# A Mamba block and a linear attention block on one core: the four taps of a depthwise convolution as products of TensorE, and shared buffers

## The reference

```python
# first block (D=256, DI=512, N=16, RANK=64, TAPS=4)
shift, scale, gate = split(silu(c) @ ada_w.T + ada_b, 3)
xn = layernorm(x) * (1 + scale) + shift
x_in, z = split(xn @ in_proj_w.T, 2)
u = silu(depthwise_causal_conv(x_in, conv_w) + conv_b)   # 4 taps along the rows
dt_r, B, C = split(u @ x_proj_w.T)
dt = softplus(dt_r @ dt_proj_w.T + dt_proj_b)
h[t] = h[t-1] * exp(dt[t] * A) + dt[t] * u[t] * B[t]     # 512 x 16 states
y = (h . C + u * D) * silu(z)
x1 = x + gate * (y @ out_proj_w.T)
# second block: linear attention with 8 heads
q, k, v = LN(x1) @ Wq, LN(x1) @ Wk, LN(x1) @ Wv
y = softmax(q, in a head) @ (softmax(k, over the rows).T @ (v * mask))
out = x1 + silu(LN(y) * (1 + s) + b) @ W_out + b_out
```

## Time and profile before

| | |
|---|---|
| median of 3 runs | 570.05 us (568.83 to 570.15) |
| the profiled execution | 569.01 us, span 567.2 us |
| mean granted TensorE clock in it | 0.901 of 2.4 GHz |
| VectorE busy | 514.6 us, 566 instructions |
| GpSimd busy | 453.0 us, 318 instructions |
| TensorE busy | 437.9 us, 2456 instructions |
| ScalarE busy | 408.6 us, 897 instructions |

### The profile page before, as it was taken

The page is one execution under the profiler, slowest core; times in us unless marked ns, Lnnn a source line. Parts: engine busy times, 40 slices in busy tenths (PEclk is TensorE's granted clock), DMA queues, the critical chain, the costliest instruction groups (busy, mean ns, idle before and its releaser), DMA issues. The chain is left out here.

```text
span 567.2 us, 7391 instructions
## 1 busy us (share of the span) xinstructions
PE 437.9 (77%) x2456; PEld 361.2 (64%) x2456; DVE 514.6 (91%) x566; ACT 408.6 (72%) x897; POOL 453.0 (80%) x318
## 2 busy tenths in 40 slices
PE   8967666769789787768688678768787777866887
PEld 7646445657676676656576667647674666755776
DVE  2479899999999999999999999999999999999753
ACT  2693677668865998578966999488966988486533
POOL 4049969989998889979998889978997989985121
PEclk8988777896789798998989898998899898779899
DMA  9294032201430044001440045011440045000001
GB/s 269 66 326 125 3 114 85 102 4 54 159 112 0 29 151 154 14 19 40 159 131 1 28 151 165 2 29 43 147 129 1 10 151 166 2 0 20 0 1 37
DMA packets 22366, 45.38 MB, mean 80 GB/s; under 512 B 3685, under 2 KB 13557, under 8 KB 22329
## 3 DMA queue, kind: packets, MB, share of 16 engines
q1 hardware_dynamic: 22328, 44.92, 24.3%
HBM read 42.52 MB, written 2.39 MB: 79 GB/s over the span
## 5 line engine op out<-in xcount | busy, mean ns | idle before, releaser
L530 POOL TENSOR_TENSOR hs<-dtu,Br 128x1024 f32<-128x1024 f32 x127 | 297.0, 2362 | 8.5 <-DMA Br<-bc_rows 8.5
L722 ACT ACTIVATE ring<-dt,Aneg 128x256 f32<-128x256 f32 x512 | 212.9, 465 | 72.6 <-DVE hs L957 68.7
L950 DVE TENSOR_TENSOR_SCAN ring<-ring,hs 128x1024 f32<-128x1024 f32 x97 | 221.4, 2282 | 5.8 <-ACT ring L722 5.4
L1298 PE MATMUL sums<-ident,hs 128*128 128x128 f32 x1024 | 150.7, 303 | 36.3 <-DVE hs L957 36.0
L1298 PEld LDWEIGHTS sums<-ident,hs 128*128 128x128 f32 x1024 | 134.4, 158 | 48.3 <-DVE hs L957 44.7
L957 DVE TENSOR_TENSOR hs<-ring,Cr 128x1024 f32<-128x1024 f32 x97 | 118.8, 1225 | 3.3
L539 POOL TENSOR_TENSOR hs<-hs,Cr 128x1024 f32<-128x1024 f32 x31 | 73.2, 2360 | 42.1 <-DVE hs L950 42.1
L950 DVE TENSOR_TENSOR_SCAN hs<-ring,hs 128x1024 f32<-128x1024 f32 x31 | 70.3, 2269 | 0.0
L1366 PE MATMUL PY<-wqkvo,xT 128*128 128x256 f32 x168 | 46.6, 428 | 0.0
L1293 PE MATMUL sums<-ident,uD 128*128 128x128 f32 x64 | 15.5, 333 | 35.2 <-DVE ygT L964 35.2
L1366 PEld LDWEIGHTS PY<-wqkvo,xT 128*128 128x128 f32 x168 | 37.5, 223 | 6.6
(11 more groups left out here) (218 smaller groups left out, 694.1 us busy)
## 6 DMA issues: line engine op xcount, KB each, us to landing
Br<-bc_rows SPq DMA_DIRECT2D x32, 512.0 KB, 5.1
Cr<-bc_rows SPq DMA_DIRECT2D x32, 512.0 KB, 4.2
xg<-in_x SPq DMA_DIRECT2D x8, 256.0 KB, 2.9
out<-fin SPq DMA_DIRECT2D x7, 256.0 KB, 4.2
hs<-in_ada_wT SPq DMA_DIRECT2D x3, 512.0 KB, 4.6
win<-in_in_wT SPq DMA_DIRECT2D x2, 512.0 KB, 6.1
hs<-in_W_emb SPq DMA_DIRECT2D x2, 512.0 KB
gate<-gate_rows SPq DMA_DIRECT2D x8, 128.0 KB, 3.1
```

Of the source, the lines that this page charges most:

```text
L530: nc.gpsimd.tensor_tensor(hs[:, g % DBUF], dtu[:, b % 2, dc, :].unsqueeze(1).to_broadcast([P, NQ, T]), Br[:, NQ * q:NQ * q + NQ, :], ALU.m ...
L722: ins = nc.scalar.activation(ring[:, g % 2, j, :], dt[:, b % 2, dc, :], ACT.Exp, scale=Aneg[:, c:c + 1])
L950: V.tensor_tensor_scan(driven if by_pool(g) else decays, decays, driven, 0.0, ALU.mult, ALU.add).then_inc(s_scan_done, 1)
L1298: ins = M(YT[:, c, :], hs[:, g % DBUF, j, P * c:P * c + P], ident[:, :], is_transpose=True, start=False, stop=(q == UPC - 1 and j == NQ - ...
```

## The change

From batch 1 on, the two x halves of `in_proj` (both are in FOLDED) make all four taps. Their weights are scaled by the taps: `wtap` has win times tap 1, 2 and 3 back, and the x part of win itself is multiplied by the last tap in place once batch 0's in_proj has read it. `conv_taps` returns at once for them, and `conv_last_tap` only adds the bias. Waits on the taps become waits on that one read. The scaling is four products on GpSimd (`scale_taps`), from a broadcast of the tap rows loaded into slots 1 and 2 of hs.

Also, vm is xh, kT is xT and fin is ke, the last batch has its vm and kT in slots of hs, and gate has one buffer. So `exp_k` waits for the store of the batch before, and SyncE issues the store of batch b - 3 between the loads of B and of C.

```diff
+FOLDED = (0, 1)
+FOLD_LO, FOLD_N = 2 * P * FOLDED[0], 2 * P * len(FOLDED)
+def folded(b, h):
+    return b >= 1 and h in FOLDED
+def taps_until(b, h):
+    return sum(3 * 2 for c in range(b + 1) for k in range(2) if not folded(c, k) and (c, k) <= (b, h))
...
-        gate = sb("gate", [P, 2, D])
+        gate = sb("gate", [P, D])
+        wtap = sb("wtap", [P, TAPS - 1, KD, FOLD_N])
-        vm = sb("vm", [P, TC, D])
-        qT, kT = sb("qT", [P, KD, T]), sb("kT", [P, TC, D])
+        vm, kT = xh, xT
+        qT = sb("qT", [P, KD, T])
-        fin = sb("fin", [P, TC, D])
+        fin = ke
+        wrow = hs[:, 1:1 + len(FOLDED)].rearrange("p s n t -> p (s n t)").rearrange("p (s e) -> p s e", s=TAPS)
...
# SyncE, broadcast_bc(b), for b >= 1
                     for q in range(UPC):
                         broadcast_b(b, q)
+                    if b >= 3:
+                        store(b - 3)
                     for q in range(UPC):
                         broadcast_c(b, q)
...
             def load_gate(b):
-                if b >= 2:
-                    sp.wait_ge(s_gated, b - 1)
+                if b >= 1:
+                    sp.wait_ge(s_gated, b)
...
+            sp.dma_start(wrow, a["tap_rows"][:, FOLD_LO:FOLD_LO + FOLD_N].unsqueeze(0).to_broadcast([P, TAPS, FOLD_N])).then_inc(
+                s_ld_taps, 16)
             broadcast_bc(0)
...
# GpSimd
+            def scale_taps():
+                pool.wait_ge(s_ld_taps, 16)
+                pool.wait_ge(s_xz_mm, 2)
+                part = win[:, :, FOLD_LO:FOLD_LO + FOLD_N]
+                for s in range(1, TAPS):
+                    nc.gpsimd.tensor_tensor(wtap[:, s - 1], part, wrow[:, s, :].unsqueeze(1).to_broadcast([P, KD, FOLD_N]),
+                                            ALU.mult).then_inc(s_taps_ready, 1)
+                pool.wait_ge(s_taps_ready, TAPS - 1)
+                nc.gpsimd.tensor_tensor(part, part, wrow[:, 0, :].unsqueeze(1).to_broadcast([P, KD, FOLD_N]),
+                                        ALU.mult).then_inc(s_taps_ready, 1)
+                pool.wait_ge(s_taps_ready, TAPS)
             for g in range(FIRST, LAST):
+                if g == -6:
+                    scale_taps()
...
# ScalarE
+                    tap = 1.0 if folded(b, h) else pcol("conv_w", TAPS * dc + 3, TAPS * dc + 4)
                     nc.scalar.activation(conv[:, dc, :], xz_bank(b, h)[:, e, :], ACT.Identity, bias=pcol("conv_b", dc, dc + 1),
-                                         scale=pcol("conv_w", TAPS * dc + 3, TAPS * dc + 4)).then_inc(s_conv0_ready, 1)
+                                         scale=tap).then_inc(s_conv0_ready, 1)
             def silu_u(b):
-                act.wait_ge(s_tap_done, 3 * DC * (b + 1))
+                act.wait_ge(s_conv0_ready, DC * (b + 1))
+                act.wait_ge(s_tap_done, taps_until(b, 1))
             def exp_k(b):
                 act.wait_ge(s_kmax_ready, b + 1)
+                if b >= 1:
+                    act.wait_ge(s_out_stored, 16 * min(b, LAST_B - 1))
...
# VectorE
             def conv_taps(b, h):
+                if folded(b, h):
+                    return
...
# TensorE
+            def wait_x_read(b, h):
+                pe.wait_ge(s_conv0_ready, DC * b + 2 * h + 2)
+                if not folded(b, h):
+                    pe.wait_ge(s_tap_done, taps_until(b, h))
...
                 elif b == 1:
                     if h >= 2:
-                        pe.wait_ge(s_tap_done, 3 * DC * b + 6 * (h - 1))
+                        wait_x_read(b, h - 2)
                 elif h <= 2:
-                    pe.wait_ge(s_tap_done, 3 * DC * b + 6 * h)
+                    wait_x_read(b, h - 1)
...
-                if h < 2:
+                if h < 2 and folded(b, h):
+                    if b == 1:
+                        pe.wait_ge(s_taps_ready, TAPS)
+                    for e in range(2):
+                        lo = P * (2 * h + e)
+                        bank = xz_bank(b, h)
+                        for s in range(TAPS):
+                            for k in range(KD):
+                                w = wtap[:, s - 1, k, lo - FOLD_LO:lo - FOLD_LO + P] if s else win[:, k, lo:lo + P]
+                                ins = M(bank[:, e, s:T], w, xnT[:, k, 0:T - s], start=(s == 0 and k == 0),
+                                        stop=(s == TAPS - 1 and k == KD - 1), skip_group_check=True)
+                elif h < 2:
```

More of the change, by code:

```diff
@@ L178, in build @@
         ve2, rs2, nb2 = sb("ve2", [P, TC]), sb("rs2", [P, TC]), sb("nb2", [P, TC])
-        fin = sb("fin", [P, TC, D])
+        fin = ke
+        last_vm, last_kT = (hs[:, s].rearrange("p n t -> p (n t)")[:, 0:TC * D].rearrange("p (c d) -> p c d", c=TC) for s in (0, 1))
         gate_dram = nc.dram_tensor("gate_rows", (NB, D), F32, kind="Internal").ap()
@@ L204, in build @@
         s_ld_post = sem("ld_post")
+        s_ld_taps = sem("ld_taps")
+        s_taps_ready = sem("taps_ready")
         s_pool_const = sem("pool_const")
@@ L301, in build @@
         b_loaded, c_loaded = [sem(f"b_loaded{q}") for q in range(UPC)], [sem(f"c_loaded{q}") for q in range(UPC)]
-        gate_loaded = [sem(f"gate_loaded{i}") for i in range(2)]
+        s_gate_loaded = sem("gate_loaded")
         s_out_stored = sem("out_stored")
@@ L342, in xT_of, with vm_of, kT_of @@
             return xnT if b == LAST_B else xT
+        def vm_of(b):
+            return last_vm if b == LAST_B else vm
+        def kT_of(b):
+            return last_kT if b == LAST_B else kT
         def xh_of(b):
@@ L398, in load_gate @@
             def load_gate(b):
-                if b >= 2:
-                    sp.wait_ge(s_gated, b - 1)
-                sp.dma_start(gate[:, b % 2, :], gate_dram[b].unsqueeze(0).to_broadcast([P, D])).then_inc(
-                    gate_loaded[b % 2], 16)
+                if b >= 1:
+                    sp.wait_ge(s_gated, b)
+                sp.dma_start(gate[:, :], gate_dram[b].unsqueeze(0).to_broadcast([P, D])).then_inc(s_gate_loaded, 16)
             def store(b):
@@ L444, in _ @@
             load_gate(0)
-            load_gate(1)
             for b in range(1, NB + 2):
@@ L448, in _ @@
                     broadcast_bc(b)
-                if b >= 3:
+                if b >= NB:
                     store(b - 3)
@@ L452, in _ @@
                     load_x(b + 2)
-                if b + 1 < NB:
-                    load_gate(b + 1)
+                if b < NB:
+                    load_gate(b)
             for c in range(TC):
@@ L968, in gate_x @@
                 dve.wait_ge(s_out_mm, b + 1)
-                dve.wait_ge(gate_loaded[b % 2], 16 * (b // 2 + 1))
+                dve.wait_ge(s_gate_loaded, 16 * (b + 1))
                 if b >= 2:
                     dve.wait_ge(s_fin_ready, b - 1)
-                V.tensor_tensor(x1[:, b % 2], PY[:, :, :], gate[:, b % 2, :].unsqueeze(1).to_broadcast([P, TC, D]),
+                V.tensor_tensor(x1[:, b % 2], PY[:, :, :], gate[:, :].unsqueeze(1).to_broadcast([P, TC, D]),
                                 ALU.mult).then_inc(s_gated, 1)
@@ L1086, in last_x1 @@
                 if c == 0:
-                    dve.wait_ge(gate_loaded[i], 16 * (b // 2 + 1))
+                    dve.wait_ge(s_gate_loaded, 16 * (b + 1))
                     dve.wait_ge(s_fin_ready, b - 1)
                     dve.wait_ge(s_xh_ready, TC * LAST_B)
-                V.tensor_tensor(x1[:, i, c], last_half(c), gate[:, i, :], ALU.mult).then_inc(s_gated, 1)
+                V.tensor_tensor(x1[:, i, c], last_half(c), gate[:, :], ALU.mult).then_inc(s_gated, 1)
                 dve.wait_ge(s_gated, LAST_B + c + 1)
```

9 lines of the change are left out of this document (5 added, 4 removed).

## The result

| | before | after |
|---|---|---|
| median | 569.73 us (568.83 to 570.15, 4 runs) | 624.22 us (621.98 to 626.06, 4 runs) |
| ratio, 95% interval | | 1.0957 (1.0918 to 1.0996) |
| span of the profiled execution | 567.2 us | 624.3 us |
| mean granted clock | 0.90 | 0.896 |
| from one gate_y of dc 3 to the next, from batch 1's to batch 5's | 63.3 to 63.7 us | 69.7, then 71.2 to 71.4 |

The change makes the kernel 54.5 us slower; 626 us had been forecast. The lines have other numbers now: L530 is L555, L722 is L764, L950 is L995, L957 is L1002, L964 is L1009, L1002 is L1047, L615 is L656, in_proj's L1242 is L1298 (L1304 in batch 0) and sum_states' L1298 is L1360.

The account below looks back on a forecast made before the run. VectorE was taken as the bound, busy 62.48 of 63.5 us a batch. Start 10.0, batch 2 5.7 and batches 3 to 7 40.0 add 55.7 to 569.0: 624.7, with 1.0 for the median 626 us; range 605 to 642 (0.68).

Parts of the forecast that it names:

- The first rival: Only one of the two stalls counts, as ScalarE's second wait finds room: 593, some 598 if gate_y slips; chance 0.10.
- the buffers and the store cost nothing: At exp_k and the reused tiles: the store lands with 5 us left, other waits stand already, so no cost.
- The pitch: TensorE's in_proj: 0.214 us an instruction of 256 columns, so 32 instructions take 7.0 us a half.
- The steady batches, 5 x 8.0 = 40.0: Blocks of batches 3 to 7: scan 3 7.3 us late and gate_y 0.7 more, 8.0 each, 40.0 in all.
- The first stall: VectorE, free since 290.9, waits at head_blocks until 297.9 for TensorE's work behind the first block: 7.0 us.
- The walk at full clock: Line-by-line timeline of one batch from the first block at 287.03: scan 3 starts at 310.8 instead of 303.54.
- gate_y's further 0.7: After scan 3, gate_y waits for unit 3's sum on TensorE, ending at 318.3: 0.7 us more a batch.
- blocks at full clock: No in_proj block counted at 1.2 GHz, where it takes 13.6 us; one in five so would give 16 us more.
- Batch 2, 5.7: Block of batch 2, without an earlier batch's attention: 5.0 us at scan 3 and 0.7 for gate_y, 5.7.
- The start, 10.0: Block of batch 1: scale_taps delays rstd0 and softplus, then the long block delays setup_emb and sums; scan 6 10.0 us late.
- VectorE's saving is in these shifts; without it they would be 39.6 more.: Over batches 1 to 7, the removed VectorE taps (L916), 39.6 us, were taken as already counted in the 55.7.
- 626 or a little under: Denser TensorE work makes half-clock stretches rarer, by the cited clock-gate rule, so 626 us or a little under.

Follow-up runs that it names:

- run 2: The changed kernel with only the first x half folded, the second half's taps left on VectorE: 598.33 us, 1.0506 of the kernel before.
- run 3: The changed kernel with only the second x half folded, the first half's taps left on VectorE: 585.48 us, 1.0280 of the kernel before.
- run 4: The changed kernel making only the last tap's products in batches 1 to 7, the other three taps missing: 565.37 us, 0.9922 of the kernel before.
- run 5: The kernel before, taps kept on VectorE, plus 24 more TensorE instructions a half into a tile nothing reads: 629.21 us, 1.1052 of the kernel before.
- run 1: The changed kernel with nothing folded and no scaling, only the shared buffers and moved store kept: 569.01 us, 0.9989 of the kernel before.
- run 6: The changed kernel with batch 1's rstd0 behind the first of the four scale_taps products: 619.20 us, 1.0873 of the kernel before.
- run 8: The changed kernel, only second half folded, run 6 and run 7 edits, conv_last_tap_1, copy_z, z blocks one unit later, out_proj behind unit 3's sum: 576.47 us, 1.0141.
- run 11: Run 9 with copy_yg also one unit later on ScalarE: 573.93 us, 1.0058 of the kernel before.
- run 9: Run 8 with conv_last_tap_1 one more unit later on ScalarE: 574.75 us, 1.0104 of the kernel before; its first expectation was 556 to 562 us.
- run 7: The changed kernel with setup_emb ahead of batch 1's in_proj on TensorE: 619.45 us, 1.0874 of the kernel before.

## Why the prediction was right, and where it was not

**The time, 626 against 624.2, and its mechanism.** Two stalls a batch behind longer blocks, at head_blocks and scan 3, both from in-order queues: shown by runs 2 to 5. The first rival (only one stall counts, 593 to 598) falls with run 3; with one half folded, run 2 gives 598. That the buffers and the store cost nothing: shown by run 1. That the total came so near is in part luck: in the span the start is 4.0 us over its term and the last batch, which had none, 1.8, while the other blocks are 3.5 under theirs and 1.0 came off between them. And in the steady batches a walk that was 1.6 us too long stands for a loss to the clock that I had put at nothing.

**The pitch.** A block of 32 instructions takes 7.1 us (178.90 to 186.0), against 7.0 worked out.

**The steady batches, 5 x 8.0 = 40.0.** Measured 37.1 (6.0, 8.1, 8.1, 8.3, 6.6). The average was near, the parts less so:
- The first stall was put at head_blocks alone, 7.0 us, with gate_y of dc 3 done at 290.9. But gate_y needs the sum of unit 15, and my walk had that sum behind the block, at 295.15, on TensorE's own line. The stall is 6.67 us, 4.50 of it one step earlier than I put it. I had copied VectorE's 290.9 from the trace of before instead of deriving it from TensorE's line above it.
- The walk at full clock was 0.9 us too long at scan 3 (22.89 after the block's start instead of 23.77), and gate_y's further 0.7 (0.6 by the walk's own 318.3 and 317.7) did not come. It would give 6.4 a batch, and batches 3 and 7 have 6.0 and 6.6.
- In the blocks of batches 4, 5 and 6 the other 1.6 to 2 us come from the clock, at a place I hadn't looked at. The timeline of batch 5's block, same steps as above:
```profile
319.77 1.13 PE L1298 MATMUL PX<-xnT,win 128*128 128x256 f32 x4
...
331.07 1.95 PE L1490 MATMUL PY<-att,qT 128*128 128x128 f32 x8 [0.70 <-DVE att L1047]
...
344.31 2.30 DVE L995 TENSOR_TENSOR_SCAN ring<-ring,hs 128x1024 f32<-128x1024 f32 x1 [6.00 <-ACT ring L764]
```
  q_times_att at L1490 takes 1.95 us, with 1.16 in batches 3 and 7, and VectorE's wait at scan 3 is 6.00 instead of 4.35. The windows above have a granted clock of 0.64 here, so most of this stretch was at the lower level of 1.2 GHz, and 1.00 in batch 3. The large blocks of batches 2 to 7 do run at the full 2.4 GHz: their 12 instructions of one kind take 2.73 us at every place. So "blocks at full clock" holds, and the price was paid by the small products behind the stall, on the same chain. Run 6 is the witness: L1490 at 1.16 in each of the five, and the batches take 69.7 to 70.3. The kernel before has slow ones too (2.08 at 293.81), where VectorE didn't wait for them.

**Batch 2, 5.7.** Measured 5.1.

**The start, 10.0.** Measured 14.0, the term with the largest error. The chain was right: scaling from 21.86 (forecast 20.3), when the tap rows have landed, to 31.26 (30.0), softplus at 33.99 (33.0), block from 42.61 (41.7) to 59.2 (57.0), setup_emb to 64.7 (62.5), gate_y 70.19 (67.5), scan 6 at 75.98 (73.7). Two sizes were short. The tap rows took 10.5 us to land, where I had some 3; as they were issued at 11.28 the scaling began only 1.6 us later than forecast, of which 0.9 reach the block. And the block had 16 instructions mostly at the lower clock, not 8: 2.07 us for the first four (1.03 at full) and 4.45 for the next twelve (2.73), 2.8 more where I had put 1.6. That makes 12.3 at scan 6. The last 1.7 is a VectorE instruction that waited for GpSimd (last section).

**"VectorE's saving is in these shifts; without it they would be 39.6 more."** This step of the prediction failed, and 39.6 itself is too large: it counts instructions that overlap at their full 0.472 us, while the group is busy 33.9 us. Run 5 puts what its removal brings at 5.0 us and run 4 at 4.4 (with the scaling's 2.8 given back, 7.2). My own walk contradicted it: it had VectorE ready for scan 3 at 306.2 and starting at 310.8 because ScalarE was late. Work put into those 4.6 us costs nothing, so taps kept would not have moved the end. The forecast didn't rest on the sentence, since it counted from the waits. The expectations of runs 4, 8 and 11, and the first one of run 9, did rest on it, and all were too fast: they priced VectorE's taps as time and not as the cover of another engine's chain.

**The rule cited for the clock.** The Trainium skill, TensorE: Matmul & The Clock Gate, section on the HAM clock gate, was quoted with "activity releases the throttle". The rows agree for the blocks. They don't show the gain that I said would follow, "626 or a little under" for rarer slow stretches: the mean clock is 0.896 against 0.90, and there are slow stretches ahead of the second blocks.

## What to carry to other kernels

Before work is moved off the bound engine, ask what that work covers: take it out altogether (a run that computes less) and see how much of its time comes back. Here 33.9 us of VectorE's work came back as 4.4, or 7.2 with the price of the scaling given back. And a block that grows on an in-order engine is paid at every step queued behind it, its own and those of the engine that reads it. When you move the reader later, walk each step behind its new place, for the wait goes there: scan 3, scan 4, copy_yg, z block.

## What the runs showed of the hardware

A VectorE instruction whose operands are all in SBUF can wait for a GpSimd product that is running, with no semaphore between them. The wait then lies in its own length, and the profile names nobody. Timeline of after, at the embedding's small steps:
```profile
80.99 9.31 POOL L555 TENSOR_TENSOR hs<-dtu,Br 128x1024 f32<-128x1024 f32 x4
...
88.36 1.97 DVE L1113 TENSOR_SCALAR m1s<-mods,par 128x8 f32<-128x8 f32 x1
...
90.24 0.22 DVE L1113 TENSOR_SCALAR m1b<-mods,par 128x8 f32<-128x8 f32 x1
```
L1113, a TENSOR_SCALAR of 128x8, takes 1.97 us where the next three take 0.22. It ends at 90.33, when the last of the four GpSimd products that began at 80.99 is over (87.93 to 90.30). In run 7 the same instruction is beside no such product and takes 0.23, and gate_y of dc 2 is 1.8 earlier. The kernel before has one such case as well: L934, a TENSOR_TENSOR of 128x256, took 1.74 us from 40.89 beside a GpSimd product from 39.98 to 42.34; the same instruction takes 0.41 in the kernel after. And run 6 has two at the start: L969 ends at 32.30 and L971 at 34.78, beside GpSimd products that end at 32.02 and 34.50.
The Trainium skill, SBUF — State Buffer, section "Who interferes with whom", says that VectorE and GpSimd share a port pair under an exclusive lock, and that a VectorE instruction with two SBUF inputs contends with a GpSimd instruction that reads SBUF. Of a VectorE instruction in a mode with two ports it says that whoever issues first gets the pair for the whole instruction and the other is fully blocked. The rows agree: each began behind a GpSimd product that was running, and ended 0.03 us (L1113) or 0.28 us (the three of 128x256) behind its end. No run here tells which of the two conditions L1113 meets. I had counted no such wait.
